# The sum of squares of a gated state-space layer moved from TensorE to VectorE turns and row copies, with one fading step placed later

## What is computed

```python
x = L0_attn_input_states                       # 2 sequences x 512 tokens x 512
proj = layernorm(x) @ in_proj_w.T              # gate, x/B/C, dt
xBC  = silu(conv4(xBC) + conv_b)               # four taps along the tokens
y    = ssd(hs, A, Bm, Cm, D, dt, dt_bias)      # 128 heads of 64, 8 groups of 16 heads
g    = y * silu(gate)
gg   = g.reshape(b, l, 8, 1024)
var  = mean(gg * gg, axis=-1)                  # one number for each token and group
g    = gg * rsqrt(var + 1e-5) * norm_w
x    = x + g @ out_w.T
x    = x + lora_ffn(layernorm(x))              # 512 -> 1376 -> 512, rank 16
```

## Time and profile before

| | |
|---|---|
| median of 3 executions | 1715.68 us (1715.34 to 1719.24) |
| the profiled execution's own time | 1716.82 us |
| its span in the trace | 1715.0 us |
| PE busy | 1696.1 us, 99% of the span |
| DVE, ACT, POOL busy | 1298.6, 1194.9, 1229.7 us |
| granted clock of PE over the span | 0.999 |

### The profile page before, as it was taken

The page is one execution under the profiler, slowest core; times in us unless marked ns, Lnnn a source line. Parts: engine busy times, 40 slices in busy tenths (PEclk is TensorE's granted clock), DMA queues, the critical chain, the costliest instruction groups (busy, mean ns, idle before and its releaser), DMA issues.

```text
span 1715.0 us, 27399 instructions
## 1 busy us (share of the span) xinstructions
PE 1696.1 (99%) x9557; PEld 1406.3 (82%) x9557; DVE 1298.6 (76%) x2200; ACT 1194.9 (70%) x2232; POOL 1229.7 (72%) x1058
## 2 busy tenths in 40 slices
PE   9999999999999999999999999999999999999999
PEld 7788888888888888888888888888888888787887
DVE  8897778868796879787986889687977799664323
ACT  6877677777877787777777777768777777663411
POOL 5586778787787778787877788777878687774610
PEclk9999999999999999999999999999999999999999
DMA  5654547464665555555746465556555564554301
GB/s 188 175 137 140 166 145 214 118 172 134 201 166 152 160 170 159 151 155 148 213 131 168 117 203 163 152 164 184 164 147 148 154 201 117 164 137 136 86 10 49
DMA packets 155176, 259.86 MB, mean 152 GB/s; under 512 B 27936, under 2 KB 56224, under 8 KB 155040
## 3 DMA queue, kind: packets, MB, share of 16 engines
q1 hardware_dynamic: 155040, 258.11, 52.4%
HBM read 229.21 MB, written 28.84 MB: 150 GB/s over the span
## 4 chain that ended last, share of the span: by engine, by line
PE 90%; DVE 5%; POOL 1%; issue 1%; DMA 1%; ACT 1%; SPq 0%; DVEq 0%; ACTq 0%; POOLq 0%
PE bank L1821 18%; PE bank L1823 17%; PE bank L1822 17%; PE bank L1899 7%; PE bank L1960 6%; PE bank L1943 6%; PE bank L1950 6%; PE bank L1914 4%; DVE ow_l L1464 2%; PE bank L2204 1%; PE bank L2206 1%; PE bank L2205 1%; PE bank L1976 1%; DVE bcT L1458 1%; PE bank L1883 1%
## 5 line engine op out<-in xcount | busy, mean ns | idle before, releaser
L771 POOL TENSOR_TENSOR w_l<-w_raw,w_h 128x512 fp32r<-128x512 f32 x288 | 397.6, 1383 | 270.2 <-ACT w_h L973 269.9
L1821 PE MATMUL bank<-x_h,w_h 128*128 128x512 f32 (+1 forms) x1328 | 527.1, 397 | 10.0 <-DVE bcT L1458 5.9
L1823 PE MATMUL bank<-x_h,w_l 128*128 128x512 f32 (+1 forms) x1328 | 519.1, 391 | 0.0
L1822 PE MATMUL bank<-x_l,w_h 128*128 128x512 f32 (+1 forms) x1328 | 518.1, 390 | 0.0
L1026 ACT ACTIVATE decay<-decay,cols 128x128 f32<-128x128 f32 x1024 | 318.3, 390 | 3.6 <-POOL decay L777 1.5
L1458 DVE SCALAR_TENSOR_TENSOR x_ch<-bank,par,x_ch 128x511 f32<-128x511 f32 (+2 forms) x384 | 286.3, 746 | 34.2 <-ACT x_ch L991 25.0
L1821 PEld LDWEIGHTS bank<-x_h,w_h 128*128 128x128 f32 (+1 forms) x1328 | 249.6, 188 | 64.1 <-issue 11.7
L1823 PEld LDWEIGHTS bank<-x_h,w_l 128*128 128x128 f32 (+1 forms) x1328 | 249.1, 188 | 54.0
L1822 PEld LDWEIGHTS bank<-x_l,w_h 128*128 128x128 f32 (+1 forms) x1328 | 249.8, 188 | 50.5
L777 POOL TENSOR_SCALAR_AFFINE_SELECT decay<-decay 128x512 f32<-128x512 f32 x256 | 200.7, 801 | 69.6 <-DMA decay<-cum_scratch 68.6
L1512 DVE TENSOR_TENSOR decay<-decay,bank 128x512 f32<-128x512 f32 x256 | 171.0, 682 | 81.6 <-ACT decay L1026 81.4
(11 more groups left out here) (164 smaller groups left out, 2775.8 us busy)
## 6 DMA issues: line engine op xcount, KB each, us to landing
w_raw<-in_wp SPq DMA_DIRECT2D x288, 256.0 KB, 3.6
decay<-cum_scratch SPq DMA_DIRECT2D x256, 256.0 KB, 4.7
ec<-ecum_scratch SPq DMA_DIRECT2D x96, 256.0 KB, 7.0
x_rows<-xt_scratch SPq DMA_DIRECT2D x46, 512.0 KB, 3.3
ow_raw<-in_ow SPq DMA_DIRECT2D x64, 256.0 KB, 5.4
xt_scratch<-xw_sq SPq DMA_DIRECT2D x124, 128.0 KB, 3.0
w_raw<-in_w SPq DMA_DIRECT2D x48, 256.0 KB, 2.8
xt_scratch<-ec_sq SPq DMA_DIRECT2D x60, 128.0 KB, 2.4
```

Source lines behind the costliest of these rows:

```text
L771: pool.tensor_tensor(w_l[:, s, :], w_raw[:, s, :], w_h[:, s, :].bitcast(F32), ALU.subtract).then_inc(wl_ready, 1)
L1821: pe.matmul(dst, wh, xh, start=(opens and k == 0), stop=False)
L1822: pe.matmul(dst, wh, xl, start=False, stop=False)
L1823: last = pe.matmul(dst, wl, xh, start=False, stop=(k == len(terms) - 1 and not more))
```

## The change

It has three parts.

1. **The sum over the channels leaves PE.** `square_total` and its 64 calls are gone, with PE's waits for `mean_ready`. In its place DVE has `turn_squares`: it transposes the folded squares in 32 x 32 blocks, sums each block's 32 channels (leaving 4 partial sums for each of 128 tokens, spread over 4 x 32 partitions), and transposes that once more. SP then copies 16 rows of 32 numbers with four small DMAs from `sq_rows` to `sq_full` (`move_squares`). `mean_square` now waits for these, transposes, adds the four parts and adds eps: three instructions for one.
2. **Places.** `turn_squares` stands behind `gated`; `mean_square` moves from ahead of `gated` to right ahead of `accumulate`; POOL's `inverse_root` moves behind the masks of the quarters 2 and 3. `move_squares` stands in SP's queue behind the loads of `ec` in a group's first slot, and behind the slot's first weight tile in the others. In the seventh slot's end and the last chunks there are like insertions (`last_chunk` of SP and DVE, `first_up` split in two).
3. **Later fading.** In a group's first slot the `fade` of the next chunk moves from ahead of the taps of B to behind them.

```diff
+            def move_squares(g, k):
+                K = g * CHUNKS + k
+                sp.wait_ge(sq_flipped, K + 1)
+                if some(K):
+                    sp.wait_ge(mean_ready, K)
+                else:
+                    sp.wait_ge(sq_clear, 2)
+                for q in range(QUADS):
+                    sp.dma_start(sq_full[q:P:SQ, :], sq_rows[q * SQ:q * SQ + QUADS, :]).then_inc(sq_moved, 16)
...
                         load_ec(gn, kn)
+                    if k == 0 and some(K):
+                        move_squares(*before)
...
                     if not first:
                         load_next_w(g, last, b, tiles[0])
+                    if k > 0:
+                        move_squares(*before)
                     if c == 1:
                         store_x(g, k + 2)
...
                     lows(tiles[:1])
-                    if some(g * CHUNKS + k):
-                        inverse_root(*((g, k - 1) if k else (g - 1, CHUNKS - 1)))
                     if k > 0:
                         mask(gn, kn, 2)
                         mask(gn, kn, 3)
+                    if some(g * CHUNKS + k):
+                        inverse_root(*((g, k - 1) if k else (g - 1, CHUNKS - 1)))
                     gT_low(g, k)
...
             def mean_square(g, k):
                 K = g * CHUNKS + k
-                dve.wait_ge(ss_done, K + 1)
-                dve.tensor_scalar(mean_sq[:, :], total_of(K), EPS, None, ALU.add).then_inc(mean_ready, 1)
+                dve.wait_ge(sq_moved, 16 * QUADS * (K + 1))
+                dve.transpose(sq_back[:, :], sq_full[:, :]).then_inc(mean_step, 1)
+                dve.wait_ge(mean_step, 2 * K + 1)
+                dve.tensor_reduce(mean_sq[:, :], sq_back[:, 0:QUADS], mybir.AxisListType.X, ALU.add).then_inc(mean_step, 1)
+                dve.wait_ge(mean_step, 2 * K + 2)
+                dve.tensor_scalar(mean_sq[:, :], mean_sq[:, :], EPS, None, ALU.add).then_inc(mean_ready, 1)
+
+            def turn_squares(g, k):
+                K = g * CHUNKS + k
+                dve.wait_ge(sum_ready, K + 1)
+                dve.transpose(y[:, 1, :], y[:, 0, :]).then_inc(sq_turned, 1)
+                dve.wait_ge(sq_turned, K + 1)
+                dve.tensor_reduce(sq_part[:, 0:QUADS], y[:, 1, :].rearrange("p (b t) -> p b t", b=QUADS),
+                                  mybir.AxisListType.X, ALU.add).then_inc(sq_summed, 1)
+                dve.wait_ge(sq_summed, K + 1)
+                if some(K):
+                    dve.wait_ge(sq_moved, 16 * QUADS * K)
+                dve.transpose(sq_rows[:, :], sq_part[:, :]).then_inc(sq_flipped, 1)
...
                         add_state(g, k)
-                        mean_square(*before)
                         gated(g, k)
+                        turn_squares(*before)
...
                     scale_x(gn, kn)
                     if not first:
+                        mean_square(*before)
                         accumulate(*before)
...
                     taps_of(tiles[1:2])
-                    if k == 0 and not first:
-                        fade(gn, kn)
...
                         taps_of(tiles[2:3])
                     if k == 0:
+                        if not first:
+                            fade(gn, kn)
                         scale_across(gn, kn)
...
                     inside(g, k)
...
-                    if not first:
-                        square_total(*((g, k - 1) if k else (g - 1, CHUNKS - 1)))
                     new_state(g, k)
```

55 lines of the change are left out of this document (31 added, 24 removed).

## The result

The changed kernel takes 1788.94 us (median of 4, 1785.73 to 1798.96), the kernel before 1715.61: a ratio of 1.0427, with a 95% interval from 1.0409 to 1.0445. It is 73 us slower, where 48 were forecast, and 4 us above the end of the range.

What follows compares the result with a forecast made beforehand. PE's queue was taken as the bound, DVE between first and second slots. First slots +35.9, second +10.9, last of a sequence +9.8, others -10.3, middle +2 summed to +48.3 us: 1764 us, range 1725 to 1785.

Steps and rivals of the forecast that it cites:

- T: DVE's `turn_squares`, two transposes and a sum with two handoffs: 0.80 us.
- M: DVE's `mean_square` with two handoffs: 0.55 us, for 0.15 before.
- R: `accumulate`, right behind the mean, waits for POOL's power: 0.75 us; before, only first slots were thought to wait.
- W: DVE's wait for the moved rows in first slots: 3.9 us each, from a landing taken at 831.
- A: First slots, 7 times: DVE has no gap and hands its delay to PE, +5.13 us each, +35.9 us.
- C: Last slots of a sequence, 14 times: POOL's `gT_l` and `xw_l` come late for PE, 0.7 us each, +9.8 us.
- B: Second slots, 8 times: `accumulate` comes 2.1 us later against 0.74 us of reserve, +1.36 us each, +10.9 us.
- Here the rows land without cost: Second slots: the queue is short and `xdt` lies between, so no wait for the moved rows was counted.
- The rest: Other slots have enough reserve and 47 keep 0.22 us, -10.3 us; the middle slot costs +2 once.
- The last four chunks: End of the kernel: PE has nearly 4 us of reserve there, so no delay was counted.
- The first rival: The rows land at once, W = 0.4 us: 1738 us, from 1725 to 1745; chance 0.20.
- The third rival: Worse than forecast, W = 5.7 us plus 12 us for clock falls in first slots: 1788 us; over 1785, chance 0.08.

Runs made afterwards that it cites:

- e2: The kernel before without its 64 small products on PE, the mean taken from one column: 1704.50 us, ratio 0.9930.
- e13: The changed kernel with the copies left out only for the seven sums that first slots take up: 1754.79 us, ratio 1.0224.
- e15: The changed kernel without any copies (e3), plus 19 small DVE transposes ahead of the mean in first slots as a fixed delay: 1757.38 us, ratio 1.0239.
- e5: The changed kernel with the four copies ahead of the two loads of `ec` in first slots: 1767.38 us, ratio 1.0291.
- e1: The kernel before with only the later fade in a group's first slot: 1718.04 us, ratio 1.0004.
- e3: The changed kernel without the 256 small copies, the sum over the four quarters left out: 1725.56 us, ratio 1.0051.
- e16: e15 plus nine idle products on PE ahead of the first `out_half` of first slots: 1757.50 us, ratio 1.0239.
- e11: The changed kernel with the copies left out for the seven sums that fifth slots take up: 1789.38 us, ratio 1.0434.
- e9: The changed kernel with nine idle products on PE ahead of the first `out_half` of a group's first slot: 1791.31 us, ratio 1.0435.
- e12: The changed kernel with the fade of the second chunk back ahead of the taps of B: 1797.18 us, ratio 1.0476.
- e10: The kernel before with the sum on DVE only in slots 3, 4, 7 and 8 of each group: 1710.09 us, ratio 0.9959.

## Why the prediction was wrong, by its own steps

**What leaves PE** held: 13.6 at most, 12.0 measured (e2).

**What DVE gets** held in size: T was forecast at 0.80 us and took 0.79 (853.89 to 854.68 above), M 0.55 and took 0.58 (861.69 to 862.27), R 0.75 and took 0.73. But that only first slots had waited for the power before was a misreading. The row of the kernel before says 30 waits:

```profile
DVE acc L1584 <- POOL rstd L826: 35.1, 30, 2.4
```

They were 1.1 us in each fourth and eighth slot and 1.8 to 2.4 in each fifth, so that R took the place of a longer wait there, and these waits rose by 12 us in all (to 47.1). DVE's busy time was to rise by 68 us and rose by 55, though the rows of the six instructions add up to 1.32 us a slot for 0.15 before, 75 us in all. Some other work counts less in the groups by line (`xdt` from `x_rows` 77.6 us for 85.5, `ow_l` 66.4 for 73.6, L1543 166.0 for L1512's 171.0) and the fade more (57.4 for 49.3); the rest I have not traced.

**First slots** held in their total, partly by luck: 40.8 us forecast, 40.0 measured. The copies make 34.1 of them (e13), where W was 27.3; all the rest makes 6, where 8.6 of A and 4.9 of C stood. The landing of 831 meant W = 3.9 us, and W was 4.6 in the mean of the seven, from 3.3 to 7.5. The reading "DVE hands every microsecond to PE" held exactly (e15). That a copy is late because of the bytes ahead of it was argued from the earlier trace rows and is shown by e5.

**Second slots** came out near, 10.9 forecast and 12.9 measured, 11.1 without any copies, but not by the path of B, which had it all at `out_half`. Sorted by the product ahead of which PE fell behind, 5.4 us were at `out_half` and 3.6 at `new_state`, where the later fade alone takes as much (3.6 in e1); the rest is spread over the taps, `inside` and `across`. The later fade, which the prediction gave nothing, took 5.9 us from second slots and gave 4.9 to first ones (e1): 1 us in sum, but a good part of each.

**The failed step is "Here the rows land without cost" and "The rest".** I had costed W at nothing wherever the slot was not a first one (but for the 2.4 us of C). Outside first slots DVE waited 65 us for the rows, and outside first and second slots e3, without the copies, gives 27 us back, about the miss of 26. Two things were left out. First, the copies themselves: four issues take 2.2 us of SP one behind the other, so that even behind little traffic the last row is there 3.2 us behind the turn (slot 35: copies from 934.53, mean at 937.70), where I had counted one landing of 2.4 us from an issue that cost nothing. In fourth and eighth slots `xdt` covers 2.3 of it and 0.9 to 1.6 are waited for. Second, in fifth slots the copies stand behind `ec` and a weight tile just as in first slots they stand behind `ec`, and there only `xdt`, 1.3 us or so, is between the turn and the mean: 4.1 us of wait in the mean of the seven. I had compared T + M + R = 2.1 with the reserve of `accumulate`, when 2.1 + 4.1 was to be compared. As the old wait for the power, 1.8 us, fell away at the same time, PE's share was 10 us. The rows for it were in the trace: in slot 36 of the kernel before, the weight tile issued behind `ec` at 913.4 took 8.6 us to land, where it had been 9.4 in the first slot.

**Last slots of a sequence** held in their path, a little too large: 9.8 us were forecast. At `new_state` PE fell behind by 2.7 us in first and 1.5 in fifth slots; without the copies it gained 1.6 and 1.8 there (e3), so late copies cost 4.3 and 3.3, 7.6 in all. The 0.22 us by which these fourteen slots start sooner were taken off in C and stand in the rest of the sum as well: 3.1 us too much gain.

**The last four chunks** were forecast at a small gain and lost 7.6 us. Behind the last chunk nothing covers the turn, the copies and the mean: PE waits 4.07 us for the normalized rows that `accumulate` leads to (0.94 in e3, nothing in the kernel before).

```profile
1638.02 0.75 PE L1894 MATMUL bank<-ident_r,sgT_r 128*128 128x128 f32 x4 [4.07 <-DVE sgT L1401]
```

"Nearly 4 us of reserve" was read at `out_half`, which the last chunk's sum doesn't feed; its reader is another one.

**The first rival** spoke of 8 KB; the four copies of 4 rows of 32 numbers are 2 KB. It was not that which decided.

**The third rival** gave 1788 us, which is the measured time, by a mechanism that is not there. It had W = 5.7 us and 12 us for the clock (its 1.7 us for one fall are 1.3 in the earlier trace rows and 0.4 in the four us behind them, where the granted clock was 0.91). The clock did fall, in five of the seven first slots; the longest, behind the wait of 7.48 us:

```profile
1248.00:1251.00 3.00, 0.46 (x1) 0.49 (x2) 1.83 (x5) 0.00 (x0) 1.97 (x2) 0.66 0.40 145
1251.00:1254.00 3.00, 3.00 (x8) 2.32 (x8) 3.00 (x3) 1.01 (x4) 3.00 (x4) 0.50 0.00 0
1254.00:1257.00 3.00, 3.00 (x11) 2.32 (x10) 2.96 (x4) 3.00 (x8) 3.00 (x3) 0.71 0.00 0
```

but e15 and e16 show for a delay of 4.5 us that such falls cost nothing. The Trainium skill, "TensorE: Matmul & The Clock Gate", section "Why this matters for your kernels", says that idle gaps between bursts of products bring the clock back to half. These windows agree as to the clock; as to the time, e16 decides. A right total is no proof of its terms.

**Copies that overtake.** Copies issued behind a load can be done before it: in slot 16 the trace's semaphore events have the last copy, issued at 470.35, done at 475.46, and the second load of `ec`, issued at 467.91, at 477.09. The Trainium skill, "DMA: Bandwidth & Descriptors", section "Queues, rings and completion order", says that completion is not first in, first out over what one engine has issued, and this agrees. The overtaking was worth 1.6 us there, and W stayed nearer to the backlog than to a free landing.

What stays open: why the waits in first slots scatter between kernels that are alike there (32, 41, 44 us in the changed kernel, e11 and e9), the place of the fade in the changed kernel (e12), and of the 9.9 us in third, fourth and sixth to eighth slots only the size, not the share of each slot, was separated from e3.

## What to carry to other kernels

A small transfer between two steps of one chain costs its issues, and everything that was issued ahead of it on the same engines; look up, for every slot it occurs in and not only for the fullest, what was issued in the microseconds before, and how much independent work the waiting engine has in between. Taking 0.24 us from the bounding engine pays only where the engine that takes the work over stands idle: four slots of eight gave 0.4% (e10), all of them cost 4.3%. Before a step is moved to a free place on its own engine, look at what the other engines do at that time (e1). Before a fall of the clock is given a price, ask whether the slower engine is waited for at all.

## What the runs showed of the hardware

Four copies of 0.5 KB take about 0.5 us each to issue, as long as loads of 256 KB (2.19 us for the four in slot 32, 1.13 us for two loads of `ec`). A sum over 32 channels for four blocks (128 to 4 elements) took 0.29 us, the transpose of 32 columns 0.21, of 128 columns 0.30. DVE's product of 1024 columns with `cdec` took 2.57 us instead of 1.65, and POOL's addition of 512 columns 2.29 instead of 1.29, where the two ran at the same time (e1). Keeping PE at idle products held its granted clock at 1.00 through a delay of DVE where it otherwise fell to 0.67, with no difference in the time (1757.50 against 1757.38 us).
